# Graph attention block: the tokens' transpose moved from TensorE to transposing DMAs

## The reference

```python
h = jnp.maximum(_layernorm(x, axis=-1), 0.0)      # x: (32, 256, 512)
q, k, v = split_heads(h @ Wq.T), split_heads(h @ Wk.T), split_heads(h @ Wv.T)
bias = (adj + adj)[:, None]
a = einsum('bhnd,bhmd->bhnm', q, k) * D ** -0.5 + bias
a = where(any(a != 0, axis=-1, keepdims=True), a, -inf)
p = softmax(a, axis=-1)                           # nan -> 0
o = einsum('bhnm,bhmd->bhnd', p, v)               # heads side by side
out = x + o @ Wo.T
```

## Time and profile before

| | us |
|---|---|
| median of 3 runs (1286.04 to 1287.17) | 1287.02 |
| the profiled execution | 1287.33 |
| its span, first to last instruction | 1285.5 |
| TensorE busy | 1245.4 (97%) |
| VectorE busy | 1114.6 (87%) |
| ScalarE busy | 1054.7 (82%) |
| GpSimd busy | 884.3 (69%) |
| one batch in the middle | 38.65 |

### The profile page before, as it was taken

The page is one execution under the profiler, slowest core; times in us unless marked ns, Lnnn a source line. Parts: engine busy times, 40 slices in busy tenths (PEclk is TensorE's granted clock), DMA queues, the critical chain, the costliest instruction groups (busy, mean ns, idle before and its releaser), DMA issues. The chain is left out here.

```text
span 1285.5 us, 43965 instructions
## 1 busy us (share of the span) xinstructions
PE 1245.4 (97%) x13104; PEld 1109.5 (86%) x13104; DVE 1114.6 (87%) x4006; ACT 1054.7 (82%) x2427; POOL 884.3 (69%) x1262
## 2 busy tenths in 40 slices
PE   4899999999999999999999999999999999999996
PEld 4788988888988888988888988888988888888885
DVE  6798889888889898889898889898889898888884
ACT  4788888888888888888888888888888888888885
POOL 1676677776677776777776777776777766777765
PEclk9999999999999999999999999999999999999999
DMA  6344554554544554554554544554544554544541
GB/s 228 84 108 119 143 122 118 143 131 116 145 122 116 145 130 114 147 122 115 147 129 114 149 121 114 148 127 114 151 119 114 150 125 115 152 118 114 135 116 57
DMA packets 90772, 163.88 MB, mean 127 GB/s; under 512 B 14976, under 2 KB 23168, under 8 KB 90752
## 3 DMA queue, kind: packets, MB, share of 16 engines
q1 hardware_dynamic: 90752, 163.64, 48.9%
HBM read 46.14 MB, written 16.78 MB: 49 GB/s over the span
## 5 line engine op out<-in xcount | busy, mean ns | idle before, releaser
L884 POOL TENSOR_TENSOR fold<-minus 128x512 f32<-128x512 f32 x256 | 327.4, 1279 | 293.6 <-DVE bounds L739 293.5
L567 ACT ACTIVATE probs<-minus,bounds 128x256 f32<-128x256 f32 x1024 | 459.5, 498 | 23.8 <-DVE bounds L739 23.8
L748 DVE TENSOR_TENSOR pT_lo<-pT_ps,pT_hi 128x512 f16<-128x512 f32 x512 | 351.3, 686 | 62.5 <-ACT pT_hi L578 59.3
L578 ACT ACTIVATE pT_hi<-pT_ps 128x512 f16<-128x512 f32 x512 | 304.9, 595 | 109.7 <-PE pT_ps L403 108.1
L739 DVE CUSTOM_DVE_ANT_0 minus<-s_ps,adj_now 128x256 f32<-128x256 f32 x1024 | 388.5, 416 | 5.9 <-ACT probs L567 4.7
L403 PE MATMUL pT_ps<-ident,probs 128*128 128x128 f32 x2048 | 307.6, 273 | 1.8 <-ACT probs L567 1.6
L328 PE MATMUL job_ps<-hT_hi,w_hi 128*128 128x256 f16 x1024 | 280.2, 274 | 1.4 <-DVE w_lo L689 0.9
L328 PE MATMUL job_ps<-hT_hi,w_lo 128*128 128x256 f16 x1024 | 279.0, 272 | 0.0
L328 PE MATMUL job_ps<-hT_lo,w_hi 128*128 128x256 f16 x1024 | 278.8, 272 | 0.0
L403 PEld LDWEIGHTS pT_ps<-ident,probs 128*128 128x128 f32 x2048 | 241.8, 140 | 19.4 <-ACT probs L567 3.0
L392 PE MATMUL s_ps<-qk_stack 96*128 96x256 f32 x1024 | 246.4, 323 | 0.7 <-DVE w_lo L689 0.7
(11 more groups left out here) (77 smaller groups left out, 2253.0 us busy)
## 6 DMA issues: line engine op xcount, KB each, us to landing
qk_stack<-qk_parts SPq DMA_DIRECT2D x768, 128.0 KB, 2.3
x_in<-x SPq DMA_DIRECT2D x32, 512.0 KB, 3.4
x_res<-x SPq DMA_DIRECT2D x32, 512.0 KB, 3.7
out<-y SPq DMA_DIRECT2D x64, 256.0 KB, 2.1
adj_in<-adj SPq DMA_DIRECT2D x32, 256.0 KB, 3.5
w_in<-wq SPq DMA_DIRECT2D x2, 512.0 KB, 6.7
w_in<-wk SPq DMA_DIRECT2D x2, 512.0 KB, 8.2
w_in<-wv SPq DMA_DIRECT2D x2, 512.0 KB, 7.9
```

Of the source, the lines that this page charges most:

```text
L567: end = nc.scalar.activation(probs[hh % 2][:, t, :], minus[hh // 2 % 2][:, hh % 2, t, :], ACT.Exp, bias=bounds[:, hh // 2 % 4, 2 * (hh % 2 ...
L578: nc.scalar.activation(pT_hi[hh % 4][:, :, :], pT_ps[hh % 2][:, :].rearrange("p (m n) -> p m n", m=NT), ACT.Copy).then_inc(pT_high, 1)
L748: nc.vector.tensor_tensor(pT_lo[hh % 4][:, :, :], pT_ps[hh % 2][:, :].rearrange("p (m n) -> p m n", m=NT), pT_hi[hh % 4][:, :, :], ALU.sub ...
L884: nc.gpsimd.tensor_tensor(f1[:, :, :], src[:, :, 0:N // 2], src[:, :, N // 2:N], ALU.add).then_inc(folded1, 1)
```

## The change

The transposes "h" leave TensorE. GpSimd now writes `h` as (x - mean) clipped at zero, without the scale. ScalarE (`split_tokens`) multiplies it by 1/std into the f16 high half, VectorE (`low_tokens`) makes the low half, both still with tokens on partitions, in one tile `h_parts` of 128 x (2 tiles) x 1024. Two transposing DMAs for each batch (`turn_tokens`), 256 KB each, turn one half of the tokens into `hT`. SP issues them for batch b + 1 between the quarters of the second stack of batch b: the first before quarter 1, the second before quarter 2; each waits until the v product that read its part of `hT` last has ended. All token work is done one batch earlier: moments of b + 2 at the end of slot 6 of batch b (before: of b + 1 in slot 0), GpSimd's h in slot 7 (before: slot 1), the split in slot 10. At the start the two turns of batch 0 stand behind the third weight load. The y pieces take slots 4 to 6 and 11 to 13, and qk pieces move with them.

```diff
-    0: [("qk", 3, 0, 0, 12)],
-    1: [("qk", 3, 0, 12, 24), ("v", 2, 0, 0, 2)],
+    0: [("qk", 3, 0, 0, 13)],
+    1: [("qk", 3, 0, 13, 24), ("v", 2, 0, 0, 2)],
...
-    4: [("h", 0, 1, 0, 4), ("y", 0, -1, 0, 6)],
-    5: [("y", 0, -1, 6, 9), ("h", 1, 1, 0, 4), ("y", 0, -1, 9, 12)],
-    6: [("qk", 0, 1, 0, 12)],
-    7: [("qk", 0, 1, 12, 24)],
-    8: [("qk", 1, 1, 0, 12)],
-    9: [("qk", 1, 1, 12, 24)],
-    10: [("qk", 2, 1, 0, 12)],
-    11: [("qk", 2, 1, 12, 24)],
-    12: [("y", 1, -1, 0, 6)],
-    13: [("y", 1, -1, 6, 12), ("o", 0, 0, 0, 4)],
+    4: [("y", 0, -1, 0, 5)],
+    5: [("y", 0, -1, 5, 10)],
+    6: [("y", 0, -1, 10, 12), ("qk", 0, 1, 0, 9)],
+    7: [("qk", 0, 1, 9, 22)],
+    8: [("qk", 0, 1, 22, 24), ("qk", 1, 1, 0, 11)],
+    9: [("qk", 1, 1, 11, 24)],
+    10: [("qk", 2, 1, 0, 13)],
+    11: [("qk", 2, 1, 13, 24), ("y", 1, -1, 0, 2)],
+    12: [("y", 1, -1, 2, 8)],
+    13: [("y", 1, -1, 8, 12), ("o", 0, 0, 0, 4)],
...
-        hT_hi = sb("hT_hi", [P, KT, N], F16)
-        hT_lo = sb("hT_lo", [P, KT, N], F16)
+        h_parts = sb("h_parts", [P, NT, 2, D], F16)
+        hT = sb("hT", [P, NT, 2 * KT, P], F16)
...
                 for j in range(G):
+                    if turned is not None and 0 < j <= NT:
+                        turn_tokens(turned, j - 1, False)
...
+            def turn_tokens(b, t, first):
+                sp.wait_ge(h_split, b + 1)
+                settled(sp, "sp")
+                if not first:
+                    sp.wait_ge(ended["v"], count("v", 2 + t, b - 1))
+                    settled(sp, "sp")
+                sp.dma_start_transpose(hT[:, t, :, :], h_parts[:, t, :, :].rearrange("p a d -> p (a d)")
+                                       ).then_inc(h_turned[t], 16)
...
+                if (i, half) == (WV, 0):
+                    for t in range(NT):
+                        turn_tokens(0, t, True)
...
-                stack(1, b, first)
+                stack(1, b, first, None if last else b + 1)
                 if not (last or isinstance(b, int) and b + 2 == B):
                     load_tokens(b + 2)
...
-                        pe.wait_ge(taken["h"], count("h", 0, b + d))
+                        for turned in h_turned:
+                            pe.wait_ge(turned, (b + (d + 1)) * 16)
...
+            def split_tokens(b, first):
+                act.wait_ge(h_ready, b + 1)
+                if not first:
+                    for turned in h_turned:
+                        act.wait_ge(turned, b * 16)
+                for t in range(NT):
+                    end = nc.scalar.activation(h_parts[:, t, 0, :], h[:, t, :], ACT.Copy, scale=rstd[:, t:t + 1])
+                end.then_inc(h_high, 1)
...
+                    if not (nearly or last) and hh == 10:
+                        split_tokens(b + 2, False)
                     if hh == HEADS - 3 and not last:
                         copy_adj(b + 1)
                     high_probs(b, hh, first and hh < 4)
...
+            def low_tokens(b):
+                dve.wait_ge(h_high, b + 1)
+                for t in range(NT):
+                    end = nc.vector.scalar_tensor_tensor(h_parts[:, t, 1, :], h[:, t, :], rstd[:, t:t + 1],
+                                                         h_parts[:, t, 0, :], ALU.mult, ALU.subtract)
+                end.then_inc(h_split, 1)
...
                     low_probs(b, hh, first and hh < 2)
-                    if not last and hh == 0:
-                        moments_of(b + 1)
...
+                    if not (nearly or last) and hh == 6:
+                        moments_of(b + 2)
+                    if not (nearly or last) and hh == 10:
+                        low_tokens(b + 2)
...
-                    end = nc.gpsimd.tensor_scalar(h[:, t, :], x_in[:, t, :], minus_mean[:, t:t + 1], rstd[:, t:t + 1],
-                                                  ALU.add, ALU.mult)
+                    end = nc.gpsimd.tensor_scalar(h[:, t, :], x_in[:, t, :], minus_mean[:, t:t + 1], 0.0,
+                                                  ALU.add, ALU.max)
...
-                    if not last and hh == 1:
-                        normalise(b + 1, False)
+                    if not (nearly or last) and hh == 7:
+                        normalise(b + 2, False)
```

More of the change, by code:

```diff
@@ L185, in attention_block @@
         rstd_ready, h_ready = sem("rstd_ready"), sem("h_ready")
+        h_high, h_split = sem("h_high"), sem("h_split")
+        h_turned = [sem(f"h_turned{t}") for t in range(NT)]
         ended = {k: sem(f"ended_{k}") for k in PER_BATCH}
@@ L217, in bank @@
         def bank(kind, n, b):
-            if isinstance(b, int) and (kind, n, b) == ("h", 1, 0):
+            if isinstance(b, int) and (kind, n, b) == ("y", 1, B - 1):
                 return 1 - BANK[kind, n]
@@ L238, in _, with stack @@
         def _(sp):
-            def stack(half, b, first):
+            def stack(half, b, first, turned=None):
                 sp.wait_ge(taken["qk"], count("qk", 2 * half + 1, b))
@@ L337, in job @@
                     begin(kind, n, d, b)
[L338 to L345, removed]
+                if kind == "qk":
                     half = PRODUCTS["qk"] // 2
                     if n == 0 and start == 0:
-                        pe.wait_ge(taken["h"], count("h", 0, b + d))
-                    if n == 0 and start <= half // 2 < stop:
-                        pe.wait_ge(taken["h"], count("h", 1, b + d))
+                        for turned in h_turned:
+                            pe.wait_ge(turned, (b + (d + 1)) * 16)
                     for i, w in enumerate((WQ, WK)):
                         if start < (i + 1) * half and stop > i * half:
-                            end = product(ps[:, i * N:(i + 1) * N],
+                            end = product(ps[:, i * N:(i + 1) * N].rearrange("p (t n) -> p t n", t=NT),
                                           [lambda k, w=m: w[:, k, n * P:(n + 1) * P] for m in (w_hi[w], w_lo[w])],
-                                          [lambda k, v=v: v[:, k, :] for v in hT], start - i * half, stop - i * half)
+                                          [lambda k, a=a: hT[:, :, a * KT + k, :] for a in range(2)],
+                                          start - i * half, stop - i * half)
                 elif kind == "v":
                     t, half = n % NT, n // NT
-                    end = product(ps[:, 0:HALF], [lambda k, v=v: v[:, k, t * P:(t + 1) * P] for v in hT],
+                    end = product(ps[:, 0:HALF], [lambda k, a=a: hT[:, t, a * KT + k, :] for a in range(2)],
                                   [lambda k, w=w: w[:, k, half * HALF:(half + 1) * HALF] for w in (w_hi[WV], w_lo[WV])],
@@ L590, in _ @@
             scale_weight(WK, 0)
-            for n in range(2):
-                take("h", n, 0)
+            split_tokens(0, True)
             high_weight(WQ, 0)
@@ L612, in _, with body @@
             exponentials(0, 0, True)
-            def body(b, first, last):
+            def body(b, first, nearly, last):
                 for hh in range(HEADS):
@@ L627, in body @@
                         take(kind, n, b + d, first and (kind, d) in (("v", 0), ("qk", 0)))
+                    if first and hh == 3:
+                        split_tokens(1, False)
+                    if not (nearly or last) and hh == 10:
+                        split_tokens(b + 2, False)
                     if hh == HEADS - 3 and not last:
@@ L775, in _ @@
             weight_scales(WK, 0)
-            for n in range(2):
-                take("h", n, 0)
+            low_tokens(0)
             low_weight(WQ, 0)
```

49 lines of the change are left out of this document (25 added, 24 removed).

## The result

The change makes the kernel slower by far more than forecast: 1591.28 us (median) against 1286.84, a ratio of 1.2379 with a 95% interval of 1.2355 to 1.2402. The direction was right; the forecast of 1439 and the upper end of the range, 1530, were not. The profiled execution has a span of 1589.5 us, 304 more than before.

A forecast was written before the change was run, and what follows sets the result against it. TensorE, busy 38.45 of 38.65 us a batch, was taken as the bound. Per batch -1.35 + 2.55 + 1.2 + 2X gives 5.0 us, 150 over 30 batches; total +152 on 1287.3: 1439 us, range 1350 to 1530.

The forecast's parts named there:

- transposes and old stall go: TensorE loses h transposes in slots 4 and 5 (1.0 us) and slot 2's wait for low halves (0.35): -1.35 a batch.
- late tokens, stall in slot 8: Tokens land at T2 + 13.3 + 2X, after VectorE reaches the moments; TensorE stalls 2.55 + 2X, 5.15 us a batch.
- split, stall in slot 12: Split of h in slot 10 makes low halves 2.38 late against 1.2 slack; TensorE stalls 1.2 us, bounds 0 and 2.4.
- batch 0, once: Batch 0 got no term of its own: one of 30 batches at 5.0 us each.
- start, once: First qk product, at 15.41 before, waits for split and two turns until 18.9: +3.5 us, 0 to 8.
- T2: Start of slot 2 in a batch, the zero from which the prediction timed stack, load and moments.
- X: How far one turning DMA pushes back what stands behind it in SP's queue: 1.3 us taken, between 0.39 and 5.2.
- the yardstick of 3.93: VectorE's stretch from first statistics instruction to the end of the next low halves, 3.93 us, used to time slot 8's stall.
- GpSimd's new h ... add nothing: GpSimd's h found ready about when ScalarE reaches the split in slot 10: no time added.
- No wait up to X = 1.5: Slot 7: the second stack's third quarter lands before head 10's scores read it at T2 + 12.25; no wait up to X = 1.5.
- slow-turn rival: Turning DMA slow in SP's queue, X above 2.6 up to 5.2, 60 us per us of X: 1517 to 1673; chance 0.11.
- lower bound for X: SP's queue: a plain DMA of 512 KB, twice the bytes, takes 0.39 us to issue, so X is at least that.

The follow-up runs named there:

- the late load alone: Kernel with both edits, batch 1's tokens in the start-up and the split tile by tile (1272.11 us), but tokens loaded behind the second stack again: 1465.73 us.
- late turn: Second turning DMA one quarter later (ahead of quarter 3), against the 1272.11 us kernel with the split tile by tile: 1362.84 us.
- both edits: Changed kernel with tokens loaded ahead of the second stack and GpSimd's h in its old add-and-multiply form, ReLU in the halves: 1320.0 us.
- the best version: Changed kernel with both edits, batch 1's tokens handled in the start-up, and the split taken tile by tile at heads 11 to 15: 1272.11 us, ratio 0.9886.

## Why the prediction was wrong, point by point

| step | forecast, us a batch | measured | by |
|---|---|---|---|
| transposes and old stall go | -1.35 | -1.57 | batch 30, its own wait on the stack taken off |
| late tokens, stall in slot 8 | +5.15 | +4.66 | the change's timeline |
| wait on the stack in slot 7 | 0 | +0.56 | the change's timeline |
| split, stall in slot 12 | +1.2 | +2.9 | the change's timeline |
| clock behind the two stalls | 0 | +2.6 | the same products in batch 30 |
| sum, with a rest of 0.2 | +5.0 | +9.4 | windows |
| batch 0, once | +5.0 | +18.0 | windows |
| start, once | +3.5 | +4.8 | first transposes of head 0 |

The direction and the largest wait were right. What failed is the sum of a batch, 5.0 against 9.7 on the mean: it had no term for the clock, took GpSimd's new h at nothing, put 1.2 on a stall that measured 2.9, and counted batch 0 as one of the 30.

- **The mechanism of the largest term was right, and its size.** T2 is 636.84 in the batch shown, so the stack starts at T2 + 1.83 (forecast 1.75); X is 1.5 (1.3). VectorE's rows below answer to the earlier trace rows: x_in is there at 653.03, T2 + 16.2, where the prediction's 13.3 + 2X gives 16.3, and the yardstick of 3.93 measures 656.13 + 0.68 - 653.03 = 3.78. With the split out of the way, the late load alone makes a stall of 5.1, where the term gives 5.55 for X = 1.5. The releaser was not the one that was named: the values stand for the factors, one step ahead of pT_lo in VectorE's queue (4.42), and only then for pT_lo (0.22); in slot 12 it is the scores that wait, for VectorE's shift.

```profile
653.03 1.29 DVE L665 BATCH_NORM_STATS2 stats<-x_in 128x6 f32<-128x512 f32 x2 [5.34 <-DMA x_in<-x]
...
656.13 0.68 DVE L769 TENSOR_TENSOR pT_lo<-pT_ps,pT_hi 128x512 f16<-128x512 f32 x1
```

- **What failed first: a stall was priced by its own length.** In the middle of the run before, at 1.00, TensorE never stands for long. But the start-up of the same trace does show what follows a long stall: behind 6.76 us of idle time TensorE is busy for 4.7 us at a granted clock of 0.50.

```profile
30.15 2.83 PE L438 MATMUL s_ps<-ident,w_in 128*128 128x128 f32 x12 [6.76 <-ACT w_in L501]
```

```profile
30.10:34.80 4.70, 4.65 (x22) 4.10 (x23) 1.76 (x5) 3.74 (x7) 0.00 (x0) 0.50 0.83 200
```

The prediction used the start-up for its start term alone and had no term for this, and the range had no room for it. In three kernels, behind late tokens, the split and a late turn, the granted clock of the stretch behind the stall is 0.54 to 0.58, and the work in it takes 1.2 to 3.0 us longer. Not every stall is followed by one: behind the 1.36 us of waits in slot 12 with both edits the batch stays at 1.00.

- **"GpSimd's new h ... add nothing" failed.** It was moved and its operation changed, and only the move was looked at. The new operation had no row, and the prediction gives no price for it; the old one took 0.77 us, the new one 2.0. That took the split's slack away. The slot-12 term held only ScalarE's and VectorE's parts, +1.2 with bounds of 0 and 2.4; the measured 2.9 is beyond the bounds, and without the slow h (both edits) the three waits of slot 12 come to 1.36, the forecast's size.
- **The low halves were priced by the wrong row.** 0.69 is the length of pT_lo, which reads one input from PSUM; the low halves of h read both from SBUF and took 1.02 on the mean in the change, while pT_lo kept 0.69.
- **"No wait up to X = 1.5" had no margin.** X came out at 1.5; the quarter was there at T2 + 12.6 instead of 12.3, and the scores wanted it 0.2 earlier than worked out.
- **Batch 0 was counted as one of the 30.** Its body handles the tokens of batches 1 and 2, and its second stack waits for batch 1's low halves; moving the tokens of batch 1 to the start-up gives back 11 us of it.
- **The rivals.** The slow-turn rival reaches to 1673 and so holds the measured time, but its cause is not there: X is 1.5, not above 2.6. Of the two rules of the Trainium skill neither holds as a price of SP's queue. By VectorE: DVE Perf Modes, section The three transpose paths, a turn of eight blocks would take 10.5 by the prediction's estimate; it took 1.5, 0.19 a block. By Advanced Engine Details and Errata, section X-Bar Transpose (TRN2), it would be as fast as a plain copy; it took SP 1.30 us against 0.52 and landed after 3.1 against 2.3. The second rule is much the nearer one. The lower bound for X, 0.39 from a load of 512 KB, was no bound for a copy inside SBUF, where a plain 256 KB cost 0.74.

Open: TensorE's 0.47 us in slot 7 and some 0.2 at the first qk product stay in the best version. A turn from another engine's queue was not tried.

## What to carry to other kernels

Price a stall of the bounding engine with what comes behind it: here the long stalls of TensorE were mostly followed by work at about half the clock, which put a quarter to three quarters of the stall's own length on top of it. Look for such a stall in the start-up too: the trace of before had one. When an operation changes its function together with its place, it needs a row of its own, whatever its shape; and work that is moved to a looser engine should be spread over slots in the smallest pieces (the same split in one slot cost 1.2 us a batch more than in two places). A move that brings a consumer forward needs its load brought forward by as much, in the issuing queue's order: one load's place cost 194 us on 1272.

## What the hardware did that I had not expected

- GpSimd's `tensor_scalar` over 128x512 f32 takes 0.69 us with add and multiply and 2.00 us with add and maximum.
- TensorE's clock, at 2.4 GHz with 1.00 granted until then, was mostly at 1.2 GHz in the rows behind idle times of 1.85 (slot 12), 2.00 (late turn), 4.4 to 4.6 (late tokens) and 6.76 us (start-up of before): granted 0.50 to 0.58, while it was busy.
- VectorE's low halves of h, with both inputs in SBUF, took 0.68 to 1.50 us, the long ones beside work of GpSimd. GpSimd can pay too: its o_raw took 0.86 us instead of 0.41 beside a low half. The Trainium skill's SBUF — State Buffer, section Who interferes with whom, says that such an instruction contends with a GpSimd instruction that reads SBUF, and that one with a single SBUF input does not (outside modes that it names). The rows agree: pT_lo, with one input in PSUM, took 0.67 to 0.70 in all runs.
- A transposing DMA of 256 KB inside SBUF held SP for 1.30 us and moved the queue back by 1.5; a plain one 0.52 and 0.74.
